# Similarity of the attention unit in one rounded pass of 96 stacked rows, with four steps moved in the order of the work

## What is computed

```python
x = x + conv(_gn(x))              # 3x3 block DCT, 192x192 product, gelu, inverse DCT
t = _to_tokens(x)                 # 16 images x 256 tokens x 192
t = t + attn(_ln_t(t))
t = t + ffn(_ln_t(t))             # 8 experts, 2 for each token

def attn(x):                      # QK = 32, hidden 384
    normed = layernorm(x) * ln_w + ln_b
    v, gate = split(silu(normed @ W_hidden.T + b_hidden))   # 384 columns each
    Z = silu(normed @ W_qk.T + b_qk)                        # 256 tokens x 32
    q = Z * gamma[0] + beta[0]
    k = Z * gamma[1] + beta[1]
    A = square(relu(q @ k.T / seq_len))                     # 256 x 256, per image
    return ((A @ v) * gate) @ W_out.T + b_out + x

def ffn(x):
    logits = x @ Wr.T                                       # 8 experts
    vals, idx = top_k(logits, 2)
    return sum over the two: softmax(vals) * (gelu(x @ Wi[e].T + bi[e]) @ Wo[e].T + bo[e])
```

## Time and profile before

| | |
|---|---|
| time, median of 3 runs (lowest, highest) | 605.21 (603.97, 606.63) |
| time of the profiled execution | 604.04 |
| its span | 602.3 |
| mean granted clock of TensorE | 0.987 of full |
| busy: TensorE, VectorE, ScalarE, GpSimd | 95%, 66%, 55%, 46% of the span |
| the second stage, from the first `attend` to the first expert product | 123.29 to 296.75 |

### The profile page before, as it was taken

One profiled execution on the slowest core, in us unless ns is written; L12 is line 12 of the kernel. 1 busy time (PEld: TensorE's weight loads), 2 busy tenths in 40 slices (PEclk: granted clock), 3 DMA queues, 4 the chain that ended last, 5 costly groups with the idle time before them and its releaser, 6 DMA issues. The chain is left out here.

```text
span 602.3 us, 14356 instructions
## 1 busy us (share of the span) xinstructions
PE 573.0 (95%) x3844; PEld 539.7 (90%) x3845; DVE 396.3 (66%) x1547; ACT 331.8 (55%) x722; POOL 275.1 (46%) x314
## 2 busy tenths in 40 slices
PE   3999999899999999999899999999999999999993
PEld 2898988778888888888799999999999999999993
DVE  4678888766877767778788555555555555555650
ACT  1522323564666776666675555556665555555651
POOL 3323231103656465565466544445555444445533
PEclk9989999998999999999999999999999999999998
DMA  8970000401111121112234333333333333333221
GB/s 288 406 307 1 0 0 2 177 2 41 54 59 59 40 72 46 59 60 68 65 97 94 54 53 53 53 43 48 54 49 50 52 47 52 46 40 40 42 27 21
DMA packets 31832, 42.45 MB, mean 70 GB/s; under 512 B 4596, under 2 KB 27797, under 8 KB 31670
## 3 DMA queue, kind: packets, MB, share of 16 engines
q0 software_dynamic: 13488, 13.74, 14.7%
q1 hardware_dynamic: 18196, 28.16, 14.2%
q10 hardware_dynamic: 114, 0.15, 0.1%
HBM read 24.46 MB, written 17.57 MB: 70 GB/s over the span
## 5 line engine op out<-in xcount | busy, mean ns | idle before, releaser
L808 ACT ACTIVATE hT<-ps,b_i_sb 128x256 f32<-128x256 f32 (+1 forms) x240 | 94.4, 448 | 113.6 <-PE ps L1332 113.5
L1332 PE MATMUL ps<-w_o_sb,hT 128*128 x852 | 145.1, 327 | 0.9 <-ACT hT L808 0.9
L1332 PEld LDWEIGHTS ps<-w_o_sb,hT 128*128 128x128 f32 x852 | 137.6, 191 | 1.3 <-issue 1.3
L694 POOL DMA_INDIRECT out_rows<-const,y_row x71 | 125.6, 1769 | 27.7 <-issue 27.7
L1332 PE MATMUL ps<-n_hi,we_hi 128*128 128x256 f32 (+1 forms) x468 | 124.7, 290 | 1.1 <-DVE we_lo L1213 1.1
L1332 PE MATMUL ps<-n_hi,we_lo 128*128 128x256 f32 (+1 forms) x468 | 92.9, 280 | 0.0
L1332 PEld LDWEIGHTS ps<-n_hi,we_hi 128*128 128x128 f32 x468 | 88.8, 190 | 1.4 <-DVE we_lo L1213 1.4
L1213 DVE TENSOR_TENSOR we_lo<-we_all,we_hi 128x768 fp32r<-128x768 f32 x80 | 73.1, 956 | 14.0 <-issue 13.1
L1332 PEld LDWEIGHTS ps<-n_hi,we_lo 128*128 128x128 f32 x468 | 71.6, 189 | 0.0
L789 ACT ACTIVATE we_hi<-we_all 128x768 fp32r x80 | 63.5, 850 | 3.8 <-DVE tile_expert L1151 2.4
L1332 PE MATMUL ps<-nA_lo,we_hi 128*128 128x256 f32 (+1 forms) x234 | 65.6, 280 | 0.0
(11 more groups left out here) (238 smaller groups left out, 1148.2 us busy)
## 6 DMA issues: line engine op xcount, KB each, us to landing
we_all<-in_w_i SPq DMA_DIRECT2D x8, 768.0 KB, 12.7
conv_only<-lists SPq DMA_DIRECT2D x31, 194.0 KB
w_o_sb<-in_w_o SPq DMA_DIRECT2D x8, 576.0 KB, 18.2
out_rows<-X SPq DMA_DIRECT2D x16, 192.0 KB
X<-in_x SPq DMA_DIRECT2D x1, 1536.0 KB, 10.4
out_rows<-const,y_row POOLq DMA_INDIRECT x71, 3.7
conv_only<-lists SPq DMA_DIRECT2D x9, 97.0 KB
we_all<-in_w_hid SPq DMA_DIRECT2D x1, 776.0 KB, 6.3
```

Source lines behind the costliest of these rows:

```text
L694: pool.indirect_dma_start(out=out, out_offset=bass.IndirectOffsetOnAxis(ap=y_row[:, odd, t:t + 1], axis=0), in_=y_sb[:, odd, t, :], in_off ...
L808: last = act.activation(hT[:, odd, f, 0:n].unsqueeze(1), ps_h[:, b, c, 0:n].unsqueeze(1), ACT.Gelu, bias=b_i_sb[:, ds(e * FCHUNKS + f, 1)])
L1332: return pe.matmul(dst, lhsT, rhs, start=start, stop=stop)
```

## The change

Four things change; nothing of the first and third stage does, but for what the list above says of the last images.

1. **Similarity.** q and k are each split into a high part (rounded to f32r) and a low remainder, and the parts are stacked to 96 rows: (q high, q high, q low) against (k high, k low, k high). One f32r product over 96 rows gives high·high + high·low + low·high. To have z three times, W_qk is stored three times side by side (`QK3 = 96` columns of the z product), and so is its bias. ScalarE makes the stacked q and k with one Identity activation each, with gamma as scale and beta as bias per partition, and a third one for the unrounded values (`query_key_high`); VectorE makes only the two low parts, by subtraction on 32 partitions each.
2. **GpSimd.** The power of image i (before: of r, at the head of the next step) stands between the two list writes of `row_a` and the two of `row_b`.
3. **ScalarE.** `normalise(i + 2)` stands ahead of z's Silu, but for the first step (i = -1), where it stays behind.
4. **VectorE and TensorE.** `choose(r)` stands behind the gated product; with it the prefix stands behind the output product on TensorE.

`weighted_b_o` shares `attnT`'s place, and `gamma` and `beta` are loaded in three copies.

```diff
-        zT, qT, kT = (xc[0:QK, ...][:, n * SEQ:(n + 1) * SEQ] for n in range(3))
+        zT, qk_full = (xc[0:QK3, ...][:, n * SEQ:(n + 1) * SEQ] for n in range(2))
+
+        Q_LOW, K_LOW = slice(2 * QK, QK3), slice(QK, 2 * QK)
+        q_parts = sb("q_parts", [QK3, SEQ], f32r)
+        k_parts = sb("k_parts", [QK3, SEQ], f32r)
...
-        weighted_b_o = sb("weighted_b_o", [P, 2, D])
+        weighted_b_o = attnT[:, :, 0:D]
...
             def attn_step(i):                                  # GpSimd
                 r = i - 1
-                if not absent(r):
-
-                    wait_alone(pool, u_var_done, r + 1, ld_const)
-                    wait(pool, u_done, r)
-                    pool.tensor_tensor(u_pow[:, :], u_var[:, :], minus_half[:, :], ALU.pow).then_inc(u_pow_done, 1)
                 if not absent(i):
...
-                    for c, rows in enumerate((row_a, row_b)):
-                        for t in range(HALVES):
-                            pool.indirect_dma_start(
...
+                    put_rows(0, row_a)
+                if not absent(i):
+
+                    wait_alone(pool, u_var_done, i + 1, ld_const)
+                    wait(pool, u_done, i)
+                    pool.tensor_tensor(u_pow[:, :], u_var[:, :], minus_half[:, :], ALU.pow).then_inc(u_pow_done, 1)
+                if not absent(r):
+                    put_rows(1, row_b)
...
+            def query_key_high(i):                             # ScalarE
+
+                wait_alone(act, z_done, i + 1, ld_const)
+                for n, dst in enumerate((q_parts, k_parts, qk_full)):
+                    last = act.activation(dst[:, :], zT[:, :], ACT.Identity, bias=gb_sb[:, 3 + n:4 + n],
+                                          scale=gb_sb[:, n:n + 1])
+                last.then_inc(qk_hi_done, 1)
...
+                if not absent(i + 2) and not (isinstance(i, int) and i < 0):
+                    normalise(i + 2)
                 if not absent(i + 1):
                     act.wait_ge(z_ps, i + 2)
                     act.activation(zT[:, :], ps_z, ACT.Silu).then_inc(z_done, 1)
-                if not absent(i + 2):
+                    query_key_high(i + 1)
+                if isinstance(i, int) and i < 0:
                     normalise(i + 2)
...
             def query_key(i):                                  # VectorE
-                dve.wait_ge(z_done, i + 1)
-                for n, dst in enumerate((qT, kT)):
-                    last = dve.tensor_scalar(dst[:, :], zT[:, :], gb_sb[:, n:n + 1], gb_sb[:, 2 + n:3 + n],
-                                             ALU.mult, ALU.add)
+                wait_alone(dve, qk_hi_done, i + 1, ld_const)
+                for parts, here in ((q_parts, Q_LOW), (k_parts, K_LOW)):
+                    last = dve.tensor_tensor(parts[here, :], qk_full[here, :], parts[here, :].bitcast(f32), ALU.subtract)
                 last.then_inc(qk_done, 1)
...
                 if not absent(r):
                     logits_of_tokens(r)
-                    choose(r)
...
                         dve.tensor_tensor(gatedT[:, lo:hi, :], ps_av[:, lo:hi, :], gateT[:, lo:hi, :],
                                           ALU.mult).then_inc(gated_done, 1)
+                if not absent(r):
+                    choose(r)
                 if last_image(r):
                     weights_low(2, 0)
...
                     for t in range(HALVES):                    # TensorE
-                        last = mm(ps_sim[:, t, :], kT[:, t * P:(t + 1) * P], qT[:, :])
+                        last = mm(ps_sim[:, t, :], k_parts[:, t * P:(t + 1) * P], q_parts[:, :])
```

More of the change, by code:

```diff
@@ L37 @@
 QK = 32
+QK3 = 3 * QK
 EXPERTS, FF = 8, 768
@@ L250, in build @@
         ln_sb = sb("ln_sb", [P, 2, 2])
-        gb_sb = sb("gb_sb", [QK, 4])
+        gb_sb = sb("gb_sb", [QK3, 6])
         b_out_sb = sb("b_out_sb", [P, D])
@@ L266, in build @@
         nB_bias = sb("nB_bias", [KBB, SEQ], f32r)
-        zT, qT, kT = (xc[0:QK, :, :, :].rearrange("p a t c -> p (a t c)")[:, n * SEQ:(n + 1) * SEQ] for n in range(3))
+        zT, qk_full = (xc[0:QK3, :, :, :].rearrange("p a t c -> p (a t c)")[:, n * SEQ:(n + 1) * SEQ] for n in range(2))
+        Q_LOW, K_LOW = slice(2 * QK, QK3), slice(QK, 2 * QK)
+        q_parts = sb("q_parts", [QK3, SEQ], f32r)
+        k_parts = sb("k_parts", [QK3, SEQ], f32r)
         hT = sb("hT", [P, 2, FCHUNKS, TWO])
@@ L643, in _, with put_rows @@
             pipeline(pool, conv_step, **CONV)
+            def put_rows(c, rows):
+                for t in range(HALVES):
+                    pool.indirect_dma_start(
+                        out=lists, out_offset=bass.IndirectOffsetOnAxis(ap=slots[:, c, t:t + 1], axis=0),
+                        in_=rows[:, t, :], in_offset=None).then_inc(scattered, 16)
             def attn_step(i):
                 r = i - 1
-                if not absent(r):
-                    wait_alone(pool, u_var_done, r + 1, ld_const)
-                    wait(pool, u_done, r)
-                    pool.tensor_tensor(u_pow[:, :], u_var[:, :], minus_half[:, :], ALU.pow).then_inc(u_pow_done, 1)
                 if not absent(i):
@@ L671, in attn_step @@
                     pool.wait_ge(slots_done, r + 1)
-                    for c, rows in enumerate((row_a, row_b)):
-                        for t in range(HALVES):
-                            pool.indirect_dma_start(
-                                out=lists, out_offset=bass.IndirectOffsetOnAxis(ap=slots[:, c, t:t + 1], axis=0),
-                                in_=rows[:, t, :], in_offset=None).then_inc(scattered, 16)
+                    put_rows(0, row_a)
[5 more added lines that the diff above has]
+                    put_rows(1, row_b)
             pool.wait_ge(ld_attn, 16 * 5)
@@ L1447, in z_product @@
                 pe.wait_ge(nB_bias_done, i + 1)
-                products(ps_z, w_qk_hi, w_qk_lo, slice(0, QK), False).then_inc(z_ps, 1)
+                products(ps_z, w_qk_hi, w_qk_lo, slice(0, QK3), False).then_inc(z_ps, 1)
             def gates(c):
@@ L1547, in attn_step @@
                     pe.wait_ge(tiles_done, 2)
-                if not absent(r):
-                    pe.wait_ge(in_row_done, r + 1)
-                    wait(pe, prefix_read, r)
-                    mm(ps_rows_before, before_bf[:, :], in_row[:, :])
-                    mm(ps_rows_all, ones_bf[:, :], in_row[:, :]).then_inc(prefix_ps, 1)
                 if not absent(i + 1):
@@ L1563, in attn_step @@
                     last.then_inc(out_ps, 1)
+                if not absent(r):
+                    pe.wait_ge(in_row_done, r + 1)
+                    wait(pe, prefix_read, r)
+                    mm(ps_rows_before, before_bf[:, :], in_row[:, :])
+                    mm(ps_rows_all, ones_bf[:, :], in_row[:, :]).then_inc(prefix_ps, 1)
             pipeline(pe, attn_step, **ATTN)
```

34 lines of the change are left out of this document (22 added, 12 removed).

## The result

The changed kernel took 615.18 us (median of 4 runs, 614.80 to 618.44) against 605.92 for the kernel before on the same chip: ratio 1.0165, 95% interval 1.0117 to 1.0213. It is slower by about 1.7%, where 601.6 was forecast and 607.5 was the upper end of the range. The profiled run after took 615.21 with a span of 613.5, that is 11.2 more than the span before; all that follows accounts for these 11.2.

The account below looks back on a forecast made before the run. TensorE was taken as the bound at 10.73 us per image, VectorE's loop at 10.15 as next. Steady images -5.8, start +3.2, image 1 to 2 -1.0, end +1.2 gave -2.4 from 604.04: 601.6 us, range 595.5 to 607.5.

Parts of the forecast that it names:

- TensorE's saving: Similarity on TensorE: two rounded products replace four float32 instructions, 1.02 us less per image, 10.73 to 9.71.
- VectorE's loop as the next bound: Second stage: VectorE's chain from one attend to the next, now with the choice, paces steady images at 10.15 us.
- The size of that loop: VectorE's terms sum to 10.21 us, 9.74 without the port meeting, 10.6 with another; 10.15 taken, 0.58 less per image.
- may be gone, or at most one such wait: VectorE's scales meeting GpSimd's addition at the shared port: without it 0.47 us goes, with one more wait 10.6.
- The three activations: ScalarE's three Identity activations for stacked q and k: about 1.6 us, bounds 1.1 to 1.9, hidden in steady images.
- The low parts: VectorE's two subtractions for q and k: 0.42 and 0.43 us, 0.85 together, without overlap.
- GpSimd's list loop: GpSimd's list writes, power, landing, `row_a` and copy: 9.44 us without the copy, 10.4 with it.
- the slower rival: GpSimd's list loop, blocked by VectorE, needs over 10.73 us and becomes the bound: 609 us, chance 0.14.
- The start: Attend of image 1 starts about 3.2 us later; TensorE's wait before it grows from 2.28 to some 5.4.
- Image 1 to 2: Attend of image 1 to that of image 2: low clock stays, TensorE's 1.0 us is won.
- The tables' images: Images 12 to 15, where VectorE also builds the table of tiles: no gain, 0.
- the end: First expert product: `choose` stands ahead of the weights it waits for, so its wait of 1.06 us grows by 1.2.

Follow-up runs that it names:

- E4: Changed kernel's orders on all engines, with the plain float32 similarity of the kernel before: 10.87 us per steady image, ratio 1.0082 to the kernel before.
- E14: Changed kernel with logits of the base between statistics and aggregation, and GpSimd's bias addition cut to one of 192 columns: 9.92 us per image, ratio 0.9936 to before.
- E13: Changed kernel with VectorE's logits of the base between the finished image's statistics and their aggregation: 10.70 us per image, ratio 1.0099 to before.
- E1: Changed kernel with the choice back ahead of the low parts on VectorE: 10.73 us per image, 612.13 us, ratio 1.015 to before.
- E5: Changed kernel with logits of the base right behind the two reads of the output product, ahead of the moments: 10.71 us per image, ratio 1.0092 to before.
- E9: Changed kernel with GpSimd's output bias addition cut to one of 192 columns: 10.69 us per image, ratio 1.0101 to before.
- E8: Changed kernel with early logits of the base, scales first in image 0's step, choice and prefix at their old places: 10.69 us per image, ratio 1.0079 to before.
- E10: Changed kernel with GpSimd's whole bias addition one image ahead, before the first list write: 10.63 us per image, ratio 1.0131 to before.
- E15: E13 with the whole bias addition one image ahead, before the first list write: 10.41 us per image, ratio 1.0026 to before.
- E7: Changed kernel with the norm's scales ahead of q and k's low parts in image 0's step: image 0 to 1 takes 13.21 us, ratio 1.013 to before.
- E16: E15 with scales first, image 0's base behind its gate, first expert's low parts ahead of the choice: 605.35 us, ratio 0.9984 to before.

## Why the prediction was wrong, step by step

- **TensorE's saving: right.** Between E4 and E14, both bound by TensorE with the same orders, lie 10.87 - 9.85 = 1.02 us per image, the 1.02 forecast. Not seen was that the moved prefix costs 0.14 of it (E4).
- **VectorE's loop as the next bound: right only in part.** All attends wait, and opening that loop in E13 and E14 moves the interval. But in each of after's ten images `diff` ends 0.03 behind GpSimd's addition: VectorE was there first and waited. So the loop that sets the pace in after runs over both engines. The last instruction of `place` ends at 217.60 and releases the first list write (218.50); writes, power, writes and addition follow each other to 225.06; then come the held `diff` and VectorE's scales, low parts, count and place, to 228.54. That is 0.90 + 6.56 + 3.48 = 10.94, and 11.04 for the image before: 10.99 on the mean. The forecast has no such loop; its loop of GpSimd goes over the landing of the lists and `row_a`.
- **The size of that loop: here the forecast failed.** The step took 10.15 between bounds of 9.74 and 10.6 (by its own terms the upper one is 10.21 + 0.47 = 10.68); it measured 10.99, over both. By terms, as means of the two images shown (forecast in brackets): gated product 3.29 (3.18), choice 1.70 (1.23), scales 0.86 (1.19), low parts 0.88 (0.85), count and place 1.57 (1.08), finish 2.71 (2.68). The choice, for which the forecast took no meeting, has it now: `diff` is 1.09 and 0.62 where it is 0.14 free. `picked` holds another, with the copy: 0.51 and 0.38, free 0.19. In every second image 0.35 of idle time stands at the end of count and place. The kernel turns its loop there, two images at a time, and VectorE's branch lies in it (times in ns, starts in us):
```profile
L183 DVEq COMPARE_BRANCH  x1: 56/56/56, 217.4 to 217.4; - x1
```
  The same idle time stands before (`X<-X,ps` at 209.21), where TensorE sets the pace and it costs nothing; the forecast's 1.08 was read from an image without it.
- **The reason in that step that failed** is "may be gone, or at most one such wait". I reckoned the meeting by the times of two engines that could pass each other by 0.2 us, for which no working is given, and put it at nothing or one wait of 0.47. They can't pass each other: `place` on VectorE releases the list writes, and the addition follows them on GpSimd, so it comes at the same point of every image. In all ten images of after, E1, E5 and E13 the addition held whichever two-operand instruction stood there: `diff`, the Newton step, or `in_first`, `chosen` and others in turn. So the meeting is no wait that is added to VectorE's loop; it is what closes the loop over both engines. The Trainium skill ("SBUF — State Buffer", SBUF: two separate sides) has the port pair locked for a whole instruction; the rows agree, since each held instruction ends 0.03 to 0.06 behind the addition's end (214.05 and 214.01; in E1 212.55 and 212.52). By that rule the forecast named the two ends of its loop, 9.74 and 10.6; the measured 10.99 lies beyond both.
- **What hid behind it.** Without the addition's meeting (E9) VectorE's loop through attend sets the pace, at 10.69, not 9.74. There q and k are late by 0.47, where the forecast had 0.2 and took none of it into its sum, and count and place take 1.50 on the mean of ten images instead of 1.08, for the copy and the loop's turn. The three activations were right (1.58 against 1.6). With the loop through attend shortened instead (E5, E13), or the choice back outside it (E1, E8), the loop over both engines stays, at 10.69 to 10.73: shorter than in after, since in most images the held instruction stands later in the order and less follows behind it. So two loops lie at about 10.7, and opening one wins 0.3. That both together carry the whole is shown by E14; that it is the meeting and not GpSimd's work, by E10, where the whole addition at another place gives 10.63.
- **The low parts: right.** 0.42 and 0.41, the second right behind the first.
- **GpSimd's list loop (the slower rival): wrong place.** In after, ScalarE's tanh, with which `row_a` begins, waits for VectorE's `diff` (0.70 at 215.38) and not for the landing, so this loop does not bind. In E15, with the addition in it, it does, at 10.42. That the forecast had 10.4 is luck: the copy is 0.50 instead of the 0.99 taken, and the addition, which it did not count, is in it. The slower side came by the port.
- **The start: right.** Image 0 to 1 cost 2.2 of a forecast 2.0; E7 gives it back by one reordering. VectorE's row at 131.88 is the wait for ScalarE's third activation, with the scales behind it:
```profile
131.88 0.42 DVE L1096 TENSOR_TENSOR q_parts<-xc,q_parts 32x256 fp32r<-32x256 f32 x1 [2.28 <-ACT xc L804]
```
  To the first attend it was +2.8 instead of 1.2, of which 1.39 come from the untouched first stage; the 1.4 that are left are near the forecast. Among the runs here the first attend lies between 122.6 and 131.3.
- **Image 1 to 2: wrong.** The 1.0 was not won: the attend of image 2 waits 0.55 as well, and that of image 1, at the low clock, took 4.74 instead of 4.47.
- **The tables' images (forecast 0) and the end (+1.2):** +1.5 and +1.7. The wait of the first expert product grew to 3.09 instead of 2.3; on VectorE the last choice is blocked too:
```profile
302.60 1.12 DVE L1107 TENSOR_TENSOR diff<-sorted_logits 128x2 f32<-128x2 f32 x1
```
  E16, with the low parts of the weights ahead of the choice, has no such wait.

What stays open: why an instruction is held from some 0.6 us ahead of the addition's start in the profile, and whether the output bias could be added on TensorE within E14's order, which was not tried. How the 1.50 of count and place in E9 divide into the copy, the turn and the rest was not measured by a run.

## What to carry to other kernels

When an edit frees the bounding engine, write out the next engine's loop from wait to wait, and count in it what an order moves into it; an instruction that was free beside the bound is paid in full inside the loop. Where VectorE releases GpSimd's work and GpSimd's work holds VectorE's next instruction, the two close a loop of their own: add up that loop too. In these runs the meeting moved along with the order, to the next two-operand instruction, and cost up to 1.5 us beyond that instruction's own time. Where two loops lie close together, a single edit shows only their distance (0.3 here); only opening both (a square of four runs) shows what carries the whole.

## What the runs showed of the hardware that was not expected

- The hold is longer than the addition: 1.66 us for an instruction of two elements per partition in E1 (0.15 alone), beside an addition of 1.01. In after, E1, E5 and E13, instructions that started some 0.6 us or less ahead of the addition's start in the profile were held until its end, in a list write that in E10 and E14 held none.
- GpSimd's copy of 128x384 takes 0.50, half of the addition of the same size (1.01), and holds as well: `picked` took 0.51 beside it, and 0.19 in the images of E14 where it started ahead of it.
- Two products of 8 columns (the prefix) cost TensorE 0.14 us per image behind the output product (E4) and nothing between attend and z, where the output product started 3.32 behind attend with them or without.
- The granted clock fell in the long wait ahead of attend 1. Its last part, with TensorE idle since 136.22:
```profile
140.00:141.57 1.57, 0.00 (x1) 0.03 (x1) 1.34 (x11) 0.80 (x3) 0.58 (x1) 0.50 0.35 125
```
  0.50 is the lower level of 1.2 GHz; the attend behind it took 4.74. In E7, without that wait, TensorE is busy for 4.95 of the 5 us and the clock is full:
```profile
139.00:144.00 5.00, 4.95 (x28) 4.34 (x27) 3.55 (x20) 4.91 (x12) 1.56 (x4) 1.00 0.00 0
```
